# Gate inputs of a recurrent layer: token loads ahead, parts in fp32r, and a second engine for half of the bias additions

## What is computed

```python
t = t + _L1_ffn_ref(_ln_t(t), L1_ffn_U_i, ...)      # _ln_t: (t - mean) / sqrt(var + 1e-5), per token
# in _L1_ffn_ref:
xi = xt @ U_i + b_i
xf = xt @ U_f + b_f
xg = xt @ U_c + b_c
xo = xt @ U_o + b_o
...
c_new = h * c + i_t * g_t
```

## Time and profile before

| | us |
|---|---|
| median of three runs | 4064.18 (4056.3 to 4067.26) |
| the profiled execution, device time | 4066.59 |
| its span in the trace | 4064.8 |
| mean granted clock of TensorE | 0.971 |
| PE busy, share of the span | 3614.2, 89% |
| DVE busy | 2862.5, 70% |
| ACT busy | 2412.4, 59% |
| POOL busy | 1261.3, 31% |
| gates stage, first DMA issue to the recurrence's first DMA issue | 3215.45 to 3476.83 |

### The profile page before, as it was taken

How to read it: one execution, slowest core, us unless ns; L and a number is a source line. 1 busy time by engine, 2 the same in 40 slices (tenths; PEclk the granted TensorE clock), 3 DMA queues, 4 the chain that set the end, 5 groups by cost and what they waited for, 6 DMA issues and landing times. The chain is left out here.

```text
span 4064.8 us, 80462 instructions
## 1 busy us (share of the span) xinstructions
PE 3614.2 (89%) x29903; PEld 2939.1 (72%) x29903; DVE 2862.5 (70%) x4169; ACT 2412.4 (59%) x6208; POOL 1261.3 (31%) x708
## 2 busy tenths in 40 slices
PE   8977888788879979999999989999999687788887
PEld 5644555455558868888888878888888544688886
DVE  1558999899947754777777746777777544677787
ACT  3546888788845545666666645666566310577776
POOL 0008999899935532000000020000000000122254
PEclk9989999999989989999999989999999899999999
DMA  4573111311123332000000030000000143544565
GB/s 126 167 218 81 42 43 44 80 42 42 40 71 105 107 100 83 17 17 17 16 17 11 12 97 17 17 17 16 17 25 13 41 139 137 161 137 136 146 209 166
DMA packets 204739, 303.61 MB, mean 75 GB/s; under 512 B 18464, under 2 KB 156576, under 8 KB 201376
## 3 DMA queue, kind: packets, MB, share of 16 engines
q1 hardware_dynamic: 195232, 291.51, 23.8%
q10 hardware_dynamic: 9216, 8.39, 0.6%
HBM read 199.18 MB, written 100.66 MB: 74 GB/s over the span
## 5 line engine op out<-in xcount | busy, mean ns | idle before, releaser
L661 POOL TENSOR_TENSOR mx_big<-mp_lvs,mx_big 128x1280 f32<-128x1280 f32 (+1 forms) x256 | 801.6, 3212 | 330.0 <-ACT mp_lvs L587 313.2
L640 DVE TENSOR_TENSOR mx_big<-mp_psL,mx_big 128x2816 f32<-128x2816 f32 (+1 forms) x256 | 785.8, 3146 | 38.4 <-PE mp_psO L532 31.4
L594 ACT ACTIVATE mp_cut<-mp_psO,mx_mask 128x128 f32<-128x128 f32 x2048 | 550.8, 404 | 143.5 <-PE mp_psO L532 113.1
L1228 PE MATMUL sv_psO<-at_v_hi,sv_p_hi 128*128 128x258 f32 x2048 | 584.2, 285 | 13.1 <-DVE sv_p_lo L1316 10.1
L532 PE MATMUL mp_psO<-mx_big,mp_pair 128*16 128x256 f32 x8192 | 500.1, 384 | 107.2 <-DVE mx_big L640 88.8
L1228 PE MATMUL sv_psO<-at_v_lo,sv_p_hi 128*128 128x258 f32 x2048 | 578.8, 283 | 0.0
L1228 PE MATMUL sv_psO<-at_v_hi,sv_p_lo 128*128 128x258 f32 x2048 | 578.5, 282 | 0.0
L1247 ACT COPY sv_S<-sv_psS 128x512 f32<-128x512 f32 x512 | 300.5, 587 | 379.1 <-PE sv_psS L1202 282.9
L532 PEld LDWEIGHTS mp_psO<-mx_big,mp_pair 128*16 128x16 f32 x8192 | 326.3, 126 | 244.4 <-DVE mx_big L640 135.8
L1291 DVE TENSOR_TENSOR sv_run<-sv_run,sv_S 128x512 f32<-128x512 f32 x448 | 316.6, 707 | 248.4 <-ACT sv_S L1247 247.6
L1316 DVE TENSOR_TENSOR sv_p_lo<-sv_S,sv_p_hi 128x512 fp32r<-128x512 f32 x512 | 353.9, 691 | 107.5 <-ACT sv_p_hi L1256 106.8
(11 more groups left out here) (218 smaller groups left out, 6979.9 us busy)
## 6 DMA issues: line engine op xcount, KB each, us to landing
re_xg<-xg SPq DMA_DIRECT2D x192, 384.0 KB, 3.3
xg<-ga_xg SPq DMA_DIRECT2D x32, 768.0 KB, 3.7
att<-mx_big SPq DMA_DIRECT2D x16, 1024.0 KB, 5.5
mx_big<-rv SPq DMA_DIRECT2D x16, 1024.0 KB, 17.7
mp_pair<-att SPq DMA_DIRECT2D x128, 128.0 KB, 2.9
fr_xr<-in_x SPq DMA_DIRECT2D x16, 512.0 KB, 4.9
fr_xl<-in_x SPq DMA_DIRECT2D x32, 256.0 KB, 4.2
rv<-fr_rvs SPq DMA_DIRECT2D x16, 512.0 KB, 2.9
```

Source lines behind the costliest of these rows:

```text
L594: ins = nc.scalar.activation(cut[:, s, c, :, h * DK:(h + 1) * DK], psO[:, c % 2, :, h * DK:(h + 1) * DK], ACT.Copy, scale=mask[:, h:h + 1])
L640: nc.vector.tensor_tensor(Z[:, c % 2, 0:m], psL[:, s, 0:D].unsqueeze(1).broadcast_to([P, m, D]), big[:, rv_slot(b, c), 0:m], ALU.mult).the ...
L661: nc.gpsimd.tensor_tensor(Z[:, c % 2, m:YC], lvs[:, s, :].unsqueeze(1).broadcast_to([P, YC - m, D]), big[:, rv_slot(b, c), m:YC], ALU.mult ...
L1228: mm = pe.matmul(psO[:, j, 0:VW], a[:, u % 2, j * P:(j + 1) * P], x[:, c, :], start=(i == 0 and e == 0), stop=(i == SC - 1 and e == len(te ...
```

## The change

Everything is inside `gates_phase`.

- `tin` has four slots; the load of pass i waits for pass i - 4 to be normalised. The first token load is issued ahead of the identity and the weights, two more ahead of the biases. In the loop the load of pass i + 3 is issued ahead of the store of pass i - 2. The moments wait for the tokens alone, PE for identity and weights, and the bias additions for the biases.
- The weights are split once into `w_hi` (three ACT copies) and `w_lo` (three DVE subtractions). The transposed tokens are split in each pass into `x_hi` (ACT copy) and `x_lo` (DVE subtraction). The products are three fp32r matmuls where one float32 matmul was.
- The order: DVE does the moments of pass i, `x_lo` of pass i - 1, normalises pass i, adds the bias of row tile 0 of pass i - 2. ACT does the root of i, `x_hi` of i - 1, and copies row tile 1 of pass i - 2 from `psG` to `raw`. PE transposes pass i - 1, then multiplies pass i - 2. POOL adds the bias to `raw`.
- The hardware loop becomes straight code, and `start_at_head` is not called.

The diff, cut: of the loop bodies the new code is shown, whose old form is in the listing above.

```diff
@@ -1355,11 +1355,15 @@
         ph = Phase(nc, stack, "ga")
         ident = ph.sb("ident", [P, P])
         w = ph.sb("w", [P, KT, GW])
+        w_hi = ph.sb("w_hi", [P, KT, GW], F32R)
+        w_lo = ph.sb("w_lo", [P, KT, GW], F32R)
         bias = ph.sb("bias", [P, GW])
         eps = ph.sb("eps", [P, 1])
-        tin = ph.sb("tin", [P, 2, U, D])
+        tin = ph.sb("tin", [P, 4, U, D])
         xl = ph.sb("xl", [P, 2, U, D])
-        xT = ph.sb("xT", [P, 2, KT, U * P])
+        x_hi = ph.sb("x_hi", [P, 2, KT, U * P], F32R)
+        x_lo = ph.sb("x_lo", [P, 2, KT, U * P], F32R)
+        raw = ph.sb("raw", [P, 2, GW])
         xg = ph.sb("xg", [P, 2, U, GW])
...
-        w_in, eps_set, passed = ph.sem("w_in"), ph.sem("eps_set"), ph.sem("passed")
-        t_in = [ph.sem(f"t_in{s}") for s in range(2)]
+        w_in, b_in, eps_set, w_hi_made, w_lo_made = (ph.sem(n) for n in "w_in b_in eps_set w_hi_made w_lo_made".split())
+        t_in = [ph.sem(f"t_in{s}") for s in range(4)]
         g_out = [ph.sem(f"g_out{s}") for s in range(2)]
-        stated, aggregated, rooted, inverted, normed, turned, xT_kept, made, biased = (
-            ph.sem(n) for n in "stated aggregated rooted inverted normed turned xT_kept made biased".split())
-        start_at_head(nc, [stated, aggregated, rooted, inverted, normed, turned, xT_kept, made, biased] + g_out)
-        loads = [(ident[:, :], ident_d)] + [(w[:, :, j * D:(j + 1) * D], k_rows(u[j])) for j in range(3)] + [
...
+                def load(i):
+                    reach(sp, normed, i - 3)
+                    sp.dma_start(tin[:, i % 4], tile_rows(t2_d, i)).then_inc(t_in[i % 4], 16)
+                load(0)
+                sp.dma_start(ident[:, :], ident_d).then_inc(w_in, 16)
+                for j in range(3):
+                    sp.dma_start(w[:, :, j * D:(j + 1) * D], k_rows(u[j])).then_inc(w_in, 16)
+                load(1)
+                load(2)
+                for j in range(3):
+                    sp.dma_start(bias[:, j * D:(j + 1) * D], bg[j].rearrange("(o n) -> o n", o=1).broadcast_to([P, D])).then_inc(b_in, 16)
+                for i in range(NT + 2):
+                    if i + 3 < NT:
+                        load(i + 3)
+                    n = i - 2
+                    if n >= 0:
+                        sp.wait_ge(biased0, n + 1)
+                        sp.wait_ge(biased1, n + 1)
+                        sp.dma_start(tile_rows(xg_d, n), xg[:, n % 2]).then_inc(g_out[n % 2], 16)
                 for s in range(2):
+                    sp.wait_ge(g_out[s], 16 * (NT // 2))
             @block.tensor
             def _(pe):
+                def turn(n):
+                    pe.wait_ge(normed, n + 1)
+                    reach(pe, x_lo_kept, n - 1)
+                    for k in range(KT):
+                        for v in range(U):
+                            mm = pe.transpose(psT[:, n % 2, (k * U + v) * P:(k * U + v + 1) * P], xl[:, n % 2, v, k * P:(k + 1) * P], ident[:, :])
+                    mm.then_inc(turned, 1)
+                def products(n):
+                    pe.wait_ge(x_lo_kept, n + 1)
+                    for v in range(U):
+                        reach(pe, (biased0, raw_kept)[v], n)
+                        for lo, hi in ((0, 512), (512, GW)):
+                            terms = [(a, b, k) for k in range(KT) for a, b in ((x_hi, w_hi), (x_hi, w_lo), (x_lo, w_hi))]
+                            for j, (a, b, k) in enumerate(terms):
+                                mm = pe.matmul(psG[:, v, lo:hi], a[:, n % 2, k, v * P:(v + 1) * P], b[:, k, lo:hi], start=(j == 0), stop=(j == len(terms) - 1))
+                        mm.then_inc(made[v], 1)
+                pe.wait_ge(w_in, 64)
+                for i in range(NT + 2):
+                    if 1 <= i <= NT:
+                        turn(i - 1)
+                    if i >= 2:
+                        pe.wait_ge(w_lo_made, 3)
+                        products(i - 2)
             @block.scalar
             def _(act):
+                def root(n):
+                    act.wait_ge(aggregated, n + 1)
+                    nc.scalar.activation(std[:, n % 2], mv[:, n % 2, :, 1:2], ACT.Sqrt, bias=eps[:, :]).then_inc(rooted, 1)
+                def keep_hi(n):
+                    act.wait_ge(turned, n + 1)
+                    reach(act, made[U - 1], n - 1)
+                    nc.scalar.copy(x_hi[:, n % 2], psT[:, n % 2, :].rearrange("p (k t) -> p k t", k=KT)).then_inc(x_hi_kept, 1)
+                def keep_raw(n):
+                    act.wait_ge(made[1], n + 1)
+                    reach(act, biased1, n - 1)
+                    nc.scalar.copy(raw[:, n % 2, :], psG[:, 1, 0:GW]).then_inc(raw_kept, 1)
                 act.wait_ge(eps_set, 1)
+                for i in range(NT + 2):
+                    if i < NT:
+                        root(i)
+                    if 1 <= i <= NT:
+                        keep_hi(i - 1)
+                    if i == 0:
+                        act.wait_ge(w_in, 64)
+                        for j in range(3):
+                            nc.scalar.copy(w_hi[:, :, j * D:(j + 1) * D], w[:, :, j * D:(j + 1) * D]).then_inc(w_hi_made, 1)
+                    if i >= 2:
+                        keep_raw(i - 2)
             @block.vector
             def _(dve):
+                def moments(n):
+                    dve.wait_ge(t_in[n % 4], n // 4 * 16 + 16)
+                    for v in range(U):
+                        ins = nc.vector.bn_stats(stats[:, n % 2, v, :], tin[:, n % 4, v])
+                    ins.then_inc(stated, 1)
+                    dve.wait_ge(stated, n + 1)
+                    for v in range(U):
+                        ins = nc.vector.bn_aggr(mv[:, n % 2, v, :], stats[:, n % 2, v, :])
+                    ins.then_inc(aggregated, 1)
+                def normalise(n):
+                    dve.wait_ge(rooted, n + 1)
+                    nc.vector.reciprocal(rstd[:, n % 2], std[:, n % 2]).then_inc(inverted, 1)
+                    dve.wait_ge(inverted, n + 1)
+                    reach(dve, turned, n - 1)
+                    for v in range(U):
+                        ins = nc.vector.tensor_scalar(xl[:, n % 2, v, :], tin[:, n % 4, v, :], mv[:, n % 2, v, 0:1], rstd[:, n % 2, v, :], ALU.subtract, ALU.mult)
+                    ins.then_inc(normed, 1)
+                def keep_lo(n):
+                    dve.wait_ge(x_hi_kept, n + 1)
+                    reach(dve, made[U - 1], n - 1)
+                    nc.vector.tensor_tensor(x_lo[:, n % 2], psT[:, n % 2, :].rearrange("p (k t) -> p k t", k=KT), x_hi[:, n % 2], ALU.subtract).then_inc(x_lo_kept, 1)
+                def add_bias(n):
+                    dve.wait_ge(made[0], n + 1)
+                    reach(dve, g_out[n % 2], n // 2 * 16)
+                    nc.vector.tensor_tensor(xg[:, n % 2, 0, :], psG[:, 0, 0:GW], bias[:, :], ALU.add).then_inc(biased0, 1)
                 nc.vector.memset(eps[:, :], LN_EPS).then_inc(eps_set, 1)
+                for i in range(NT + 2):
+                    if i < NT:
+                        moments(i)
+                    if 1 <= i <= NT:
+                        keep_lo(i - 1)
+                    if i < NT:
+                        normalise(i)
+                    if i == 0:
+                        for j in range(3):
+                            dve.wait_ge(w_hi_made, j + 1)
+                            nc.vector.tensor_tensor(w_lo[:, :, j * D:(j + 1) * D], w[:, :, j * D:(j + 1) * D], w_hi[:, :, j * D:(j + 1) * D],
+                                                    ALU.subtract).then_inc(w_lo_made, 1)
+                        dve.wait_ge(b_in, 48)
+                    if i >= 2:
+                        add_bias(i - 2)
+            @block.gpsimd
+            def _(pool):
+                pool.wait_ge(b_in, 48)
+                for n in range(NT):
+                    pool.wait_ge(raw_kept, n + 1)
+                    reach(pool, g_out[n % 2], n // 2 * 16)
+                    nc.gpsimd.tensor_tensor(xg[:, n % 2, 1, :], raw[:, n % 2, :], bias[:, :], ALU.add).then_inc(biased1, 1)
```

More of the change, by code:

```diff
@@ L1395, in _ @@
             def _(sp):
[L1396 to L1406, removed]
@@ L1411, in _ @@
             @block.tensor
             def _(pe):
[L1413 to L1422, removed]
-                        n = i - 4
-                        pe.wait_ge(xT_kept, HEAD + n + 1)
-                        for u in range(U):
-                            pe.wait_ge(biased, HEAD + (n - 1) * U + u + 1)
-                            for lo, hi in ((0, 512), (512, GW)):
-                                for k in range(KT):
-                                    mm = pe.matmul(psG[:, u, lo:hi], xT[:, s, k, u * P:(u + 1) * P], w[:, k, lo:hi], start=(k == 0), stop=(k == KT - 1))
-                            mm.then_inc(made, 1)
@@ L1431, in _ @@
-                pe.wait_ge(w_in, 16 * len(loads))
-                iterations(pe, body)
+                def turn(n):
[14 more added lines that the diff above has]
```

(36 more changed lines are left out.)

22 lines of the change are left out of this document (8 added, 14 removed).

## The result

| | before | changed |
|---|---|---|
| median | 4063.4 us (4056.3 to 4067.3, 4 runs) | 3975.6 us (3972.9 to 3977.9, 4 runs) |
| ratio | | 0.9786, 95% interval 0.9773 to 0.9798 |
| profiled execution, span | 4064.8 us | 3973.6 us |
| last store of attention to the recurrence's first DMA issue | 267.8 us | 177.2 us |

The forecast was 3974, range 3962 to 3998. The last line of the table is the stage with the gaps on both sides. Its 90.6 us are all but 0.6 of the 91.2 us by which the profiled execution became shorter.

What follows compares the result with a forecast made beforehand. Gates was taken as bound by a load issued one pass late. First products 3229.9, plus products 131.8, transposes 13.5, clock 2.6, tail 3.05 end at 3380.8 instead of 3471.9: gain 91, forecast 3974 us, range 3962 to 3998.

Steps and rivals of the forecast that it cites:

- The bound before: Gates stage: a load issued one pass too late sets 7.32 us a pass, where PE needs 5.6.
- the load ring: Gates pass before the change: closed loop of load landing 3.89 us, moments 1.17, bias 1.82, queue 0.86.
- The new products: PE, each gates pass: 12 matmuls of 512 columns and 12 of 256 take 4.12 us, with transposes 4.57.
- The head: Start of gates stage: first products at 3229.9 instead of 3236.47, 6.6 us earlier, bounds 3 and 10.
- The clock: TensorE at the start of the gates stage: 2.6 us lost to half clock, bounds 1.1 and 3.9.
- The tail: After the last gates matmul: 0.2, `raw` 0.8, POOL 1.9, hops 0.15, so 3.05 us to the store.
- What is late next: New gates pass set out engine by engine: PE sets the pace at 4.57 us; DVE has 0.7 in hand.
- a ring over two passes: Transposes, `x_lo`, normalise, bias, then products: 0.3 us in hand; each us beyond costs PE half a us a pass.
- The signs: Right: PE idle below 10 us, first products near 3230; wrong: PE waits every pass, 512-column matmuls over 0.24 apart.
- Rival 2: DVE and POOL block each other at SBUF: normalising waits for POOL's 1.9 us, 0.8 a pass, 4000 us; chance 0.04.
- Rivals 1, 3, 4, 5, 6: DVE/ACT set pace 3990, 0.16; late store 3994, 0.04; half clock 4120, recurrence repeated 4161, products no faster 4088, each 0.02.

Runs made afterwards that it cites:

- five copies more: Changed kernel with five more ACT copies of the transposed tokens, into an unread buffer, ahead of `x_hi` in each pass: 4033.9 us, ratio 0.9924.

## Why the prediction was right, point by point

- **The bound before, and the load ring.** Right, and both halves were tested alone: loads ahead gave 55 us (the prediction's 1.7 a pass x 32), products alone nothing in the steady pass (4.3 us in the stage).
- **The new products.** 4.12 forecast. From the first product at 3303.90 to the next transposes it is 4.29: matmuls of 512 columns start 0.23 apart, of 256 0.12, and the first one behind the transposes takes 0.32. The transposes take 0.36, not 0.43. Together 4.65 against 4.57, 2.5 us too little in all. The rows from the attention stage carried over; the 215.7 ns for 512 columns that the prediction gave from the Trainium skill (TensorE: Matmul & The Clock Gate, "Wait — 56ns, not 53.3ns?") were not reached: 225 to 236 here.
- **The head.** The stage's first DMA issue comes 5.09 us after attention's last store, not 6.43: taken as the semaphore block, that is 1.34, forecast 1.0. No run drops the block alone, but the three kernels that have it need 6.43 to 6.48 us there, the eleven without it 5.08 to 5.11. First DMA issue to first product: 14.25, forecast 15.4; the first tokens were there 2.7 us after their issue (3213.76 to 3216.45), where I had taken a later load's 3.9. DVE did wait for the biases ahead of the moments of pass 1, 1.3 us.
- **The clock.** First pass of products 5.83 us (3228.01 to 3233.84), 1.7 more than the forecast's 4.12 and 1.5 more than the 4.29 of a later pass; forecast 2.6. That the sum is right to within 1 us is partly luck: the first product is 1.5 us early, the clock costs 0.9 less, the pace 2.5 more, and these cancel.
- **The tail.** From 0.12 behind the start of the last matmul to the last store issue 2.95, forecast 3.05. POOL's addition 1.85, forecast 1.9.
- **What is late next: the step that failed.** The prediction named a ring over two passes with 0.3 us in hand, in which each us costs half. It did have a slack of about this size, but in another place and at the full price: the ring over one pass through moments and root. I had followed `x_hi` back to the transposes only, and not to the instruction ahead of it in ACT's queue. It cost the forecast nothing, as nothing was added to that ring; five copies more would have been 1.96 us a pass where the forecast's ring says 1.3.
- **The signs.** None of those of being wrong came. The first products were at 3228.0 and the last ended at 3377.6, where 3230 and 3378 stood. One sign of being right was missed: PE was to idle for less than 10 us inside the stage, and idles for 12.4, 6.5 ahead of the first transposes (3213.76 to 3220.28) and 5.9 ahead of the second, all of it in the head.
- **Rival 2, DVE and POOL.** The mechanism is real, and my reason against it was wrong. I argued from the duration that normalising is not in the fast mode and so cannot be held; it is held in every steady pass, 0.90 us for the pair instead of 0.74. What kept it cheap is not the kind of instruction but its place: `x_lo`, which is not held, stands ahead of it, so only the last 0.4 us of POOL's instruction are met. Without `x_lo` there the pair takes 1.93. The rule that the prediction quoted (the Trainium skill, SBUF — State Buffer, "Who interferes with whom") agrees: a `tensor_scalar` waits for the whole rest of GpSimd's instruction.
- **Rivals 1, 3, 4, 5, 6.** None came: PE has no wait in the steady part, the clock is 1.00, and `re_hc` still stands 192 times. Matmuls of 512 columns start 0.23 us apart. Stores land in 3.9 us (4.6 at most), loads in 4.2, at 223 GB/s.

## What to carry to other kernels

When two bounds lie one behind the other, test each edit alone before crediting it: here the products in parts were worth next to nothing by themselves and 30 us behind the other. Follow a ring through what stands ahead in each engine's queue, not only through data; a small operation for the next pass (a root of 0.3 us) ahead of a copy for this one made a ring of a whole pass. Before a second engine is brought in to take work off a full one, look at whether the full one is working or waiting.

## What the runs showed of the hardware beyond that

- Three kinds of DVE instruction that read only SBUF (`tensor_scalar`, `tensor_copy`, `tensor_tensor` of 256 columns), started while a POOL addition with 1.46 us to go was under way, last 1.60 to 1.74 us instead of 0.29 to 0.43 and end 0.15 to 0.28 us behind POOL's. With one operand in PSUM a `tensor_tensor` keeps its time, and `bn_stats` and the reciprocal do too, although they read only SBUF.
- `tensor_scalar` of 256 columns with two constants takes 0.29 us, with its two scalars from SBUF 0.41; held, it lasts 1.61 with constants as with a scalar from SBUF. So 0.41 says nothing on whether it can be held.
- Nine matmuls whose result is thrown away (18 records, from 3225.18), put where PE would wait, had the granted clock at 1.00 when the products began at 3229.55.
- The kernels with a block that only sets eleven or twelve semaphores start the stage 1.3 to 1.4 us later than those without.
